# Graph attention with a residual norm: the targets' rows of heads 1 to 6 spread by transfers in place of transposes

## The reference

```python
h = (x @ W).reshape(n, H, C)
alpha_s = einsum('nhc,hc->nh', h, a_s);  alpha_d = einsum('nhc,hc->nh', h, a_d)
e = leaky_relu(alpha_s[src] + alpha_d[dst], 0.2)
e = exp(e - segment_max(e, dst)[dst])
alpha = e / (segment_sum(e, dst)[dst] + 1e-16)
out = segment_sum(h[src] * alpha, dst)
```

## Time and profile before

| what | value |
|---|---|
| median of 3 runs | 641.99 us |
| the profiled execution's own time | 641.79 us |
| its span on the core | 640.0 us |
| TensorE / VectorE / ScalarE / GpSimd busy | 99% / 83% / 53% / 33% |
| granted TensorE clock | 0.999 of full speed |
| one head from 3 to 6, start to start | 68.4 us |

### The profile page before, as it was taken

The page is one execution under the profiler, slowest core; times in us unless marked ns, Lnnn a source line. Parts: engine busy times, 40 slices in busy tenths (PEclk is TensorE's granted clock), DMA queues, the critical chain, the costliest instruction groups (busy, mean ns, idle before and its releaser), DMA issues.

```text
span 640.0 us, 9306 instructions
## 1 busy us (share of the span) xinstructions
PE 632.6 (99%) x3426; PEld 543.9 (85%) x3426; DVE 529.6 (83%) x928; ACT 336.3 (53%) x570; POOL 208.1 (33%) x122
## 2 busy tenths in 40 slices
PE   9999999999999999999999999999999999999996
PEld 5766568989888898989899988999898989887885
DVE  8999997889989878758684858797689868789876
ACT  7899982546524645444353635363455344534382
POOL 1000000140743824067404940375207540451230
PEclk9999999999999999999999999999999999999999
DMA  8422503125144323042302520270307130500002
GB/s 317 161 75 75 160 15 99 50 54 194 51 147 146 127 99 99 1 153 95 100 1 72 175 59 16 75 227 23 97 20 237 65 100 5 192 26 1 1 2 99
DMA packets 22173, 59.36 MB, mean 93 GB/s; under 512 B 2544, under 2 KB 2800, under 8 KB 22128
## 3 DMA queue, kind: packets, MB, share of 16 engines
q1 hardware_dynamic: 21984, 58.69, 28.2%
q10 hardware_dynamic: 144, 0.07, 0.0%
HBM read 54.03 MB, written 4.72 MB: 92 GB/s over the span
## 4 chain that ended last, share of the span: by engine, by line
PE 89%; DVE 9%; issue 0%; ACT 0%; DMA 0%; ACTq 0%
PE O L1289 31%; PE R L1184 9%; PE R L1190 9%; PE R L1187 9%; PE R L1256 6%; PE R L1262 6%; PE R L1259 6%; DVE ohd L709 3%; PE O L1201 3%; DVE ohs L713 2%; PE R L1206 1%; DVE junk L749 1%; PE O L1256 1%; PE O L1262 1%; PE O L1259 1%; PE O L1434 1%
## 5 line engine op out<-in xcount | busy, mean ns | idle before, releaser
L1111 POOL TENSOR_TENSOR W2l<-Wr,W2h 128x768 fp32r<-128x768 f32 x48 | 92.6, 1948 | 126.1 <-ACT W2h L425 126.1
L1184 PE MATMUL R<-W1h,xTh 128*128 128x384 f32 x312 | 106.3, 341 | 0.0
L1115 POOL TENSOR_TENSOR Pl<-L,Ph 128x512 fp32r<-128x512 f32 x34 | 55.5, 1651 | 153.8 <-ACT Ph L474 153.6
L1187 PE MATMUL R<-W1l,xTh 128*128 128x384 f32 x312 | 105.4, 338 | 0.0
L1190 PE MATMUL R<-W1h,xTl 128*128 128x384 f32 x312 | 105.4, 338 | 0.0
L1105 POOL TENSOR_TENSOR W1l<-Wr,W1h 128x768 fp32r<-128x768 f32 x30 | 58.8, 1970 | 129.3 <-ACT W1h L414 128.9
L749 DVE CUSTOM_DVE_ANT_0 junk<-h,abc 128x768 bf16<-128x768 f32 x64 | 64.0, 999 | 27.8 <-ACT h L437 26.7
L1289 PE MATMUL O<-W2h,gh 128*128 128x256 f32 (+1 forms) x384 | 78.5, 339 | 0.0
L1289 PE MATMUL O<-W2h,gl 128*128 128x256 f32 (+1 forms) x384 | 77.4, 336 | 0.0
L1289 PE MATMUL O<-W2l,gh 128*128 128x256 f32 (+1 forms) x384 | 77.4, 336 | 0.0
L1256 PE MATMUL R<-Ph,hh 128*128 128x512 f32 x168 | 66.3, 395 | 0.0
(11 more groups left out here) (186 smaller groups left out, 1186.2 us busy)
## 6 DMA issues: line engine op xcount, KB each, us to landing
Wr<-in_W SPq DMA_DIRECT2D x101, 384.0 KB, 3.6
abc<-in_as SPq DMA_DIRECT2D x9, 384.0 KB, 5.5
abc<-in_ad SPq DMA_DIRECT2D x9, 384.0 KB, 5.3
h_rows<-h SPq DMA_DIRECT2D x8, 384.0 KB, 2.4
hl<-h_rows SPq DMA_DIRECT2D x8, 384.0 KB, 6.0
xin<-in_xT SPq DMA_DIRECT2D x6, 256.0 KB, 5.8
xr<-in_x SPq DMA_DIRECT2D x1, 1536.0 KB, 6.7
out<-res SPq DMA_DIRECT2D x4, 384.0 KB, 2.3
```

The costliest lines, as they stand in the source:

```text
L1111: e.tensor_tensor(W2l[:, m % N2, :], Wr[:, n, :], W2h[:, m % N2, :].bitcast(f32), ALU.subtract).then_inc(s_w2l, 1)
L1115: e.tensor_tensor(Pl[:, t, d0:d1], L[:, t, d0:d1], Ph[:, t, d0:d1].bitcast(f32), ALU.subtract).then_inc(s_Pl, 1)
L1184: e.matmul(bank[:, 0:HALF], xTh[:, f, xs], hi[:, ws], start=f == 0, stop=False)
L1187: e.matmul(bank[:, 0:HALF], xTh[:, f, xs], lo[:, ws], start=False, stop=False)
```

## The change

For heads 1 to 6 the 8 transposes of the targets go. In their place SyncE stores r12 (1024 numbers of 4 bytes) to a row of 1024 numbers in DRAM, waits for that store, and loads each half of the row back with a broadcast to 128 partitions into a new SBUF buffer `rows` (2 KB a partition and half). ScalarE and VectorE then read `rows` in place of PSUM banks; they wait for the landing of the two loads. Heads 0, 7 and layer 2 keep the transposes.

With it the orders change. SyncE loads W1 blocks of the next head ahead of the last block of W2, and has the store between the loads of W1 blocks 4 and 5, the two broadcast loads behind W1 block 5. ScalarE casts W1 blocks 2 to 4 ahead of the scores, and inside the scores W1 block 5 and W2 block 5; GpSimd follows that order. In C(0) the six groups go in one pass, since the banks of head 1's targets are free. RING loses two entries a head. CT is held in 16-bit integers in place of 32-bit floats.

```diff
-        CT = sb("CT", [128, NT, N], f32)
+        CT = sb("CT", [128, NT, N], u16)
+        rows = sb("rows", [128, 2, N], f32)
...
+        tr = nc.dram_tensor("t_rows", (H, 2 * N), f32, kind="Internal").ap()
...
+        def row_ready(h, i):
+            return ((s_tr1, s_tr2)[i % 2], 16 * h) if 0 < h < H - 1 else bc_value(h, i)
+        def row_bank(h, i):
+            return rows[:, 2 - i, :] if 0 < h < H - 1 else ring_bank(("r2", "r1")[i - 1], h, 0)
...
+            def store_rows(h):
+                e.wait_ge(s_r12, 2 * h + 2)
+                with nc.allow_non_contiguous_dma(reason="columns to rows"):
+                    e.dma_start(tr[h, :].rearrange("(i t p) -> p i t", i=2, t=NT), r12[:, :, :]).then_inc(s_ts, 16)
+
+            def spread_rows(h):
+                e.wait_ge(s_ts, 16 * h)
+                if h > 1:
+                    e.wait_ge(s_L, NT * h)
+                    e.wait_ge(s_lk, NT * h)
+                e.dma_start(rows[:, 1, :], tr[h:h + 1, N:2 * N].broadcast_to([128, N])).then_inc(s_tr2, 16)
+                e.dma_start(rows[:, 0, :], tr[h:h + 1, 0:N].broadcast_to([128, N])).then_inc(s_tr1, 16)
...
             load_raw("w2", 1, 1)
+            store_rows(1)
             store_h(2, 1)
             load_raw("w2", 1, 2)
+            spread_rows(1)
             reload_h(1)
...
-            for k in range(N2, FT):
-                load_raw("w2", 1, k)
+            load_raw("w2", 1, 4)
+            store_rows(2)
+            load_raw("w2", 1, 5)
+            spread_rows(2)
...
-                load_raw("w2", h - 1, 4)
                 if h + 1 < H:
                     load_raw("w1", h + 1, 0)
                     load_raw("w1", h + 1, 1)
-                load_raw("w2", h - 1, 5)
+                load_raw("w2", h - 1, 4)
+                if h + 1 < H:
+                    load_raw("w1", h + 1, 2)
...
                 if h + 1 < H:
-                    for k in range(2, FT):
-                        load_raw("w1", h + 1, k)
+                    load_raw("w1", h + 1, 3)
+                    load_raw("w1", h + 1, 4)
+                    store_rows(h)
+                    load_raw("w1", h + 1, 5)
+                    spread_rows(h)
+                load_raw("w2", h - 1, 5)
...
                     high_w2(h - 1, 4)
-                    high_w2(h - 1, 5)
-                    scores(h, h, 0, NT, ring_bank("r2", h, 0), (gl_value(h - 1, FT - 1), (s_g, FT * h)), 3 * h + 2,
-                           lambda u, h=h: high_w1(h + 1, 1 + u) if h + 1 < H and 1 <= u <= 4 else None)
+                    if h + 1 < H:
+                        for k in range(2, 5):
+                            high_w1(h + 1, k)
+
+                    def last_rows(u, h=h):
+                        if u == 1 and h + 1 < H:
+                            high_w1(h + 1, 5)
+                        if u == 2:
+                            high_w2(h - 1, 5)
+                    scores(h, h, 0, NT, row_bank(h, 1), (gl_value(h - 1, FT - 1), (s_g, FT * h)), row_ready(h, 1), last_rows)
...
-                if n == 5:
-                    e.wait_ge(s_y, 2)
-                    targets(1, 0, NT, (ring_bank("r2", 1, 0), ring_bank("r1", 1, 0)), 4)
...
-                    if c == (0 if h == 2 else 1 if h == H - 1 else 2) and h > 1:
+                    if c == 1 and h == H - 1:
                         targets(h, 0, NT, (None, None), 2 * h + 2)
```

More of the change, by code:

```diff
@@ L40, in gat_resnorm_kernel @@
         LOADS += [("w2", h - 1, k) for k in range(4)] + [("v", H - 1, k) for k in V_ROWS.get(h, ())]
-        LOADS += [("w2", h - 1, 4)] + [("w1", h + 1, k) for k in range(2) if h + 1 < H]
-        LOADS += [("w2", h - 1, 5)] + [("v", H - 1, k) for k in V_SCORES.get(h, ())]
-        LOADS += [("w1", h + 1, k) for k in range(2, FT) if h + 1 < H]
+        LOADS += [("w1", h + 1, k) for k in range(2) if h + 1 < H] + [("w2", h - 1, 4)]
+        LOADS += [("w1", h + 1, 2) for _ in range(1) if h + 1 < H] + [("v", H - 1, k) for k in V_SCORES.get(h, ())]
+        LOADS += [("w1", h + 1, k) for k in range(3, FT) if h + 1 < H] + [("w2", h - 1, 5)]
     LOADS += [("w2", H - 1, k) for k in range(FT)]
@@ L59, in gat_resnorm_kernel @@
         if h < H:
-            RING += [("B", h, n) for n in range(4, 8)] + [("as", h, 0), ("r2", h, 0), ("r1", h, 0)]
+            RING += [("B", h, n) for n in range(4, 8)] + [("as", h, 0)]
+        if h == H - 1:
+            RING += [("r2", h, 0), ("r1", h, 0)]
     RING += [("al", H, 0), ("at", H, 0), ("as", H, 0), ("r2", H, 0), ("r1", H, 0), ("tail", 0, 0)]
@@ L549, in head_2 @@
                     evict_B(2, 0, u // 2 - 1)
-            scores(0, 0, 0, NT, ring_bank("r2", 0, 0), (), 2, head_2)
+            scores(0, 0, 0, NT, row_bank(0, 1), (), row_ready(0, 1), head_2)
             evict_B(2, 1, 0)
@@ L576, in scalar_program @@
                     scaled_as(2, 24)
-                    scores(2, 2, 0, NT, ring_bank("r2", 2, 0), (gl_value(1, FT - 1), (s_g, 2 * FT)), 8, lambda u: high_w1(3, 3 + u) if u in (1, 2) else None)
+                    scores(2, 2, 0, NT, row_bank(2, 1), (gl_value(1, FT - 1), (s_g, 2 * FT)), row_ready(2, 1), lambda u: high_w1(3, 3 + u) if u in (1, 2) else None)
                     high_h(2, 0)
@@ L932, in vector_program @@
             sums_h(1, 3, h32[:, 1, :], abc[:, 1, :, :])
-            scores(0, 0, 0, NT, ring_bank("r1", 0, 0), 3)
+            scores(0, 0, 0, NT, row_bank(0, 2), row_ready(0, 2))
             e.wait_ge(s_sd, 2)
@@ L958, in vector_program @@
                     sums_2(2)
[L959 removed]
+                    scores(1, 1, 0, NT, row_bank(1, 2), row_ready(1, 2))
                     sums_P(1, lambda: sums_2(3))
@@ L964, in vector_program @@
                 if h == 2:
-                    scores(2, 2, 0, NT, ring_bank("r1", 2, 0), 9)
+                    scores(2, 2, 0, NT, row_bank(2, 2), row_ready(2, 2))
                     sums_P(2, lambda: low_h(2, 0))
@@ L1034, in vector_program @@
             maxima(H, 0, NT, ring_bank("as", H, 0))
-            scores(H, H, 0, NT, ring_bank("r1", H, 0), 27)
+            scores(H, H, 0, NT, row_bank(H, 2), row_ready(H, 2))
             for t in range(NT):
@@ L1361, in tensor_program @@
                         half_B(h, n // 2, n % 2, take("B", h, n))
-                if h == 1:
-                    for c in range(2):
-                        stage_C(0, c, groups=range(4), ends=False)
-                    for c in range(2):
-                        stage_C(0, c, groups=(4, 5))
-                for c in range(2 if h == 1 else 0, FT):
+                for c in range(FT):
                     if c == FT - 1 and 2 <= h < H - 1:
```

24 lines of the change are left out of this document (14 added, 10 removed).

## The result

The changed kernel takes 708.89 us (median of 4 runs, 707.11 to 710.08) beside 642.05 for the kernel before on the same chip: ratio 1.104, 95% interval 1.1016 to 1.1064. It is slower by 66.8 us, and the forecast of 650.3 with its range up to 664 missed it. The profiled execution took 710.08 us, 708.3 of them in its span; its mean granted clock was 0.954.

The account below looks back on a forecast made before the run. TensorE, busy 99% of the span, bounds the kernel. Transposes -5.27 us, stalls in heads 3 to 6 +12.6 and head 2 +1.0 make +8.3 on 641.79, 650.1, plus 0.2 for the median: 650.3 us, range 637.5 to 664.

Parts of the forecast that it names:

- the forecast's own sum: Whole kernel: -5.27 us for transposes, +12.6 for stalls in heads 3 to 6, +1.0 for head 2, together +8.3.
- X: Store's landing plus load's landing, one behind the other, ahead of the scores: 7.2 us, between 4.5 and 13.7.
- X, the landing of the store: The store's part of X: SyncE's store of r12 to DRAM lands in 3.6 us, between 2.4 and 9.7.
- the high end's price: Store's upper bound: 0.131 us a packet in the busy queue, 64 packets an engine, giving 9.7 us.
- The very slow store: Rival at the store: packets cost near 0.131 us whatever they carry, X 13.3, stalls 37 us, about 675 us; chance 0.08.
- The load: Broadcast load of the rows behind the store: lands in 3.6 us, between 2.1 and 4.0.
- When the store starts: Store follows r12, taken at the old times (347.91 us in head 4, 416.27 in head 5); 0.6 added in heads 5, 6.
- The stall at B(h+1, 2): TensorE waits for the eviction behind the scores: 2.85 us each in heads 3, 4 and 3.45 in heads 5, 6.
- The chain of the scores: ScalarE's first score to the first eviction's end: left at 13.41 us, bounds -2.0 and +3.8 a head.
- Head 1: Between scores and A(1), 19 us of cover hide X and SyncE's reload of h: no cost.
- Head 2: X hidden; slower line 814 against 1.20 us of slack stalls B(3, 2) by 1.0 us, between 0.3 and 2.6, could be 0.
- The counts: 16-bit CT, in line 820 and the accumulation: taken as no gain, the accumulation at most -2.5 us.

Follow-up runs that it names:

- the kernel with all three mended: Changed kernel with 32-byte store runs, ScalarE's casts of W1 blocks 2 to 4 behind r12, and TensorE's waits in heads 3 to 6 filled with unread matmuls: 650.55 us.
- its own experiment: Changed kernel with ScalarE's cast of W1's block 5 moved from between the first scores to ahead of them: 709.52 us, ratio 1.1032.
- the mended kernel: Changed kernel with the store as 128 runs of 32 bytes and ScalarE's casts of W1's blocks 2 to 4 behind r12, before any filling: 655.19 us.
- the kernel with the wide store: Changed kernel with each partition's 8 values stored as one run of 32 bytes, 128 packets in place of 1,024: 665.36 us, ratio 1.0359.
- the 16-bit run: The kernel before with the counts kept in 16 bits and nothing else changed: 641.88 us, ratio 1.0000.

## Why the prediction was wrong

The direction and the place were right, the size was not. The runs, each mending one thing more, divide the 66.8 us so: 43.5 the store's landing, 10.2 the late r12, 4.6 the clock behind the stalls that are left, and 8.5 remain in the kernel with all three mended (650.55). Of these the forecast's own sum with the measured X of 6.5 gives 5.5, longer waits give 1.7 and the filling that ran too long 1.7; heads 1 and 2 came out some 0.5 better than their terms (C(2) starts 1.2 us earlier than in the kernel before, where the sum has 0.75).

- *X, the landing of the store*: **the step that failed.** Its bounds were 2.4 and 9.7 us and 3.6 was taken, "in the lowest sixth, because the nearest row is the store in the same direction and each packet carries 4 bytes, not 3 KB". It took 8.9 to 11.8. The step reasoned from how long a packet keeps an engine busy to when the store lands. By busy time "that price is mostly bytes" even holds, for a packet of 4 bytes is busy for some 7 ns; but the landing went by the count, at 0.10 to 0.19 us a packet, and the trace shows no packet at work in most of it. That the high end's price, 0.131 us, lies within those two is luck, since it is the busy time of packets that are mostly 3 KB. The very slow store had a chance of 0.08, and the range left it out; its 675 us was still 34 short. The estimate of 2.9 us from the Trainium skill (VectorE: DVE Perf Modes, section The three transpose paths) is contradicted by the landings of 8.9 to 11.8 us. So is the 2.0 us from the 10.5 ns of the Trainium skill (DMA: Bandwidth & Descriptors, section Measured), which that section gives as a busy span; the busy time here is of that size, but it is no price of the landing.
- *The load*: 3.6 taken, 4.2 to 5.9 on the chain of heads 3 to 6, above the high end of 4.0. That 4.0 was the shortest broadcast load of line 286 in the kernel before, whose 18 landed in 4.0 to 8.8, median 5.4: the low end of its kind stood as the high end.
- *When the store starts*: r12 was taken to be done as before. The change's new order puts GpSimd's low parts beside the four steps that make it. The forecast saw that line 814's two SBUF operands would meet GpSimd, and even that GpSimd would move ahead of the scores, but not that the steps ahead of the store have two SBUF operands as well. This cost 10.2 us once the store was short.
- *The stall at B(h+1, 2)*: right in place and mechanism; the part at W1's block 5 was not foreseen and, by its own experiment, adds nothing.
- *The chain of the scores*: right as a sum, 13.2, 13.3, 14.1 and 13.2 us in heads 3 to 6 against 13.41, but partly by luck: line 862, with both operands in SBUF, took 1.24 us on average where line 814 had taken 0.75, and the rest of the chain, with two casts fewer in it, was shorter by as much.
- *What a stall costs beyond itself*: missing. The waits of 2.7 and 3.4 us also lowered the granted clock; this is 4.6 us or somewhat more in the mended kernel, and in head 4 of the changed one 16 matmuls at 0.32 in place of 0.175 us, 2.3 us.
- *Head 1*: "nothing" was wrong, though the text said that X would show if the cover were gone; the long store used it up. *Head 2*: right in place, with a stall of 0.3 us at B(3, 2) in the kernel with the wide store, the low end of its bounds, where 1.0 was taken (the 0.37 us a step called a mean there comes from a median). *The counts*: right, as the 16-bit run shows.

## What to carry to other kernels

Count packets before bytes, and do not take the engines' busy time for the landing: a column that went out as single numbers kept them busy for 4% of the time until it landed, yet each packet put 0.10 to 0.19 us on the landing, and the transfer behind it on the queue paid too; lay it out so that a partition writes one run, or turn it first. When a change reorders one engine's work, look at what that engine's new neighbours in time do to steps ahead of the change. A transfer that replaces work on the bounding engine must fit into the slack of the consumer that waits first; move that consumer out of the way before trying it.

## What was not expected of the hardware

A store of 4 KB in 1,024 packets took 11.36 us to land with the DMA engines busy for 4% of that time and nothing else on the queue, and a load of 384 KB issued behind such a store took 12.62 us. With store and load out together the engines were 80% busy at 18 GB/s. VectorE steps on 128 x 4 numbers took 1.8 us each beside GpSimd's subtractions and 0.16 without them. Behind an idle stretch of 3.4 us in head 6 TensorE was granted half its clock for 6 us, behind an equal one in head 5 for about half as long, and behind one of 2.0 us its full clock.
